# Dense products in pieces of 32 columns, and another order of all work, in a hybrid transformer kernel

## The reference

```python
x = x + s4_block(ln(x))      # gates i, f, o, s = products 256x256; h = f*h + i*s over all tokens; y = o*h; ln
x = x + ffn(ln(x))           # r = sigmoid(xr @ Wr.T); k = relu(xk @ Wk.T)**2; r * (k @ Wv.T); token shift
x = x + attention(ln(x))     # q, k, v, out: 256x256; 16 heads of 16; causal softmax over 4096 keys
x = x + ffn(ln(x))           # the same weights again
```

```python
scores = q @ k.T / 4; scores[key > query] = -inf
p = softmax(scores - scores.max(-1)); out = p @ v
```

## Time and profile before

| | before |
|---|---|
| median of 3 runs | 1784.84 us (1783.78 to 1785.69) |
| the profiled execution | 1785.71 us, span 1783.9 us |
| PE busy | 1742.3 us, 98% |
| DVE busy | 1533.4 us, 86% |
| ACT busy | 1312.9 us, 74% |
| POOL busy | 615.0 us, 34% |
| instructions | 34777, of them 12872 MATMUL |
| granted PE clock | full in nearly all slices |

### The profile page before, as it was taken

One profiled execution on the slowest core, in us unless ns is written; L12 is line 12 of the kernel. 1 busy time (PEld: TensorE's weight loads), 2 busy tenths in 40 slices (PEclk: granted clock), 3 DMA queues, 4 the chain that ended last, 5 costly groups with the idle time before them and its releaser, 6 DMA issues.

```text
span 1783.9 us, 34777 instructions
## 1 busy us (share of the span) xinstructions
PE 1742.3 (98%) x12872; PEld 761.8 (43%) x12872; DVE 1533.4 (86%) x3040; ACT 1312.9 (74%) x2660; POOL 615.0 (34%) x927
## 2 busy tenths in 40 slices
PE   8999999999999999999999999999999999999998
PEld 8766655533445433443433443433232333323214
DVE  6685994799999999999999998999999999999802
ACT  3345465588685678778688777688979788887894
POOL 4257868714337432333501524402010222120001
PEclk9999999999999999999999999999999999999999
DMA  4232121200002000020000002100002000000000
GB/s 110 59 65 53 34 49 39 53 11 18 24 12 53 29 12 6 19 47 6 23 6 13 7 24 29 29 6 1 1 25 28 17 12 7 13 2 8 1 1 12
DMA packets 56956, 43.01 MB, mean 24 GB/s; under 512 B 8788, under 2 KB 56788, under 8 KB 56788
## 3 DMA queue, kind: packets, MB, share of 16 engines
q1 hardware_dynamic: 54548, 39.75, 9.4%
q10 hardware_dynamic: 2240, 1.05, 0.4%
HBM read 24.00 MB, written 16.25 MB: 23 GB/s over the span
## 4 chain that ended last, share of the span: by engine, by line
PE 69%; DVE 19%; ACT 6%; issue 3%; POOL 2%; DMA 0%; ACTq 0%; SPq 0%; DVEq 0%; POOLq 0%
PE psum L1690 20%; DVE span_max L1433 14%; PE psum L1637 12%; PE psum L1669 12%; PE psum L1490 11%; PE psum L1496 10%; ACT probs L1188 3%; PE psum L1484 2%; ACT probs L1199 2%; PE psum L1699 1%; PE psum L1644 1%; DVE rows L1372 1%; DVE small L1290 1%; PE psum L1652 0%; POOL small L924 0%
## 5 line engine op out<-in xcount | busy, mean ns | idle before, releaser
L1433 DVE TENSOR_REDUCE span_max<-psum 128x1 f32<-128x512 f32 (+3 forms) x2304 | 1317.5, 639 | 84.0 <-PE psum L1637 57.7
L1188 ACT ACTIVATE probs<-psum 128x512 f32<-128x512 f32 (+3 forms) x2054 | 994.4, 572 | 144.2 <-PE psum L1669 138.2
L1690 PE MATMUL psum<-probs,v_aug 128*17 128x512 f32 (+3 forms) x4608 | 566.0, 563 | 1.9 <-POOL probs L1068 1.0
L1637 PE MATMUL psum<-k_stack,q_stack 48*128 48x512 f16 (+3 forms) x2304 | 515.7, 363 | 6.9 <-DVE span_max L1433 4.2
L1669 PE MATMUL psum<-q_stack,k_stack 50*128 50x512 f16 (+3 forms) x2304 | 516.9, 365 | 5.5 <-ACT probs L1199 1.2
L1669 PEld LDWEIGHTS psum<-q_stack,k_stack 50*128 50x128 f16 x2304 | 141.4, 93 | 436.5 <-ACT probs L1188 278.9
L1637 PEld LDWEIGHTS psum<-k_stack,q_stack 48*128 48x128 f16 x2304 | 160.1, 94 | 249.3 <-DVE span_max L1433 169.6
L1068 POOL TENSOR_SCALAR_AFFINE_SELECT probs<-probs 128x512 f32<-128x512 f32 x128 | 81.5, 642 | 429.8 <-ACT probs L1188 287.9
L1690 PEld LDWEIGHTS psum<-probs,v_aug 128*17 128x17 f32 x4608 | 76.6, 95 | 140.0 <-issue 119.1
L1199 ACT ACTIVATE probs<-psum 128x1024 f32<-128x1024 f32 (+3 forms) x125 | 116.4, 969 | 19.5 <-PE psum L1669 19.1
L1107 ACT ACTIVATE rows<-psum,cols 128x256 f32<-128x256 f32 x128 | 53.6, 470 | 91.3 <-PE psum L1490 90.9
(11 more groups left out here) (134 smaller groups left out, 1575.3 us busy)
## 6 DMA issues: line engine op xcount, KB each, us to landing
q_stack<-q_parts SPq DMA_DIRECT2D x192, 32.0 KB, 2.0
k_stack<-k_parts SPq DMA_DIRECT2D x42, 128.0 KB, 4.8
rows<-in_x SPq DMA_DIRECT2D x16, 256.0 KB, 2.8
q_parts<-rows SPq DMA_DIRECT2D x32, 128.0 KB, 1.9
k_parts<-rows SPq DMA_DIRECT2D x32, 128.0 KB, 2.0
out<-rows SPq DMA_DIRECT2D x16, 256.0 KB, 2.1
x_rows<-rows SPq DMA_DIRECT2D x14, 256.0 KB, 2.2
rows<-x_rows SPq DMA_DIRECT2D x14, 256.0 KB, 2.7
```

Source lines behind the costliest of these rows:

```text
L1188: act.activation(probs[:, tile % PROBS, i, q0:], bank(b)[:, q0:], ACT.Exp, scale=SCALE / QK_SCALE).then_inc(exp_done, 1)
L1433: nc.vector.tensor_reduce(span_max[:, s % SPAN_RING, row:row + 1, k0 // SPAN:k0 // SPAN + 1], bank(b)[:, 0:k1 - k0], AX.X, ALU.max).then_i ...
L1637: ins = nc.tensor.matmul(bank(b)[:, 0:k1 - k0], q_stack[row:row + SCORE_ROWS, s % Q_RING, u, qt * P:(qt + 1) * P], k_stack[row:row + SCORE ...
L1690: ins = nc.tensor.matmul(pv_bank[32 * h:32 * h + VW, q0:], v_aug[:, j, g * HG + h, :], probs[:, tile % PROBS, h, q0:], start=(j == 0), sto ...
```

## The change

1. In `channels_out` and `tokens_out` each product with 128 weight columns becomes four products with 32, each into its own 32 partitions of the same bank. The moving operand, the result and the number of bytes read for each product stay; it is read by four instructions in place of one. 896 products become 3584 (in MATMUL records 1792 become 7168).
2. `DIVISION` tells the planner that the products now have P V's shape.
3. The numbers of the planner change, and with them the order on every engine. `AHEAD` and `LEAD` become so large that they no longer hold anything back; `MAX_AHEAD` stays 2. `TOGETHER` is 0: two banks are taken at once only if both are ready.

```diff
+COLUMNS = 32
-MOST = {"max": 4, "scores": 5, "job": 5}
-KEPT = 1
+MOST = {"max": 4, "scores": 6, "job": 4}
+KEPT = 2
-AHEAD = 36199
-LEAD = 18.25
-NEAR = 0
-SOON, TWO = 0, -3100
+AHEAD = 1273693
+LEAD = 129438.363
+NEAR = -4100
+SOON, TWO = 0, -3700
-WORTH = {"max": 3000, "dve": 1.6, "scores": 2950, "act": 1.953, "half": -2700, "pv": 1200, "stay": -11650,
+WORTH = {"max": 2957.1, "dve": 1.615, "scores": 2300.4, "act": 1.51376, "half": -12007.3, "pv": -8025.2,
...
-TOGETHER = 100
+TOGETHER = 0
-DIVISION = {"shift": "pv"}
+DIVISION = dict.fromkeys(("shift", "f", "i", "s", "o", "r", "k", "kv", "q", "kk", "v", "proj"), "pv")
             def channels_out(b, w, src, e):
                 for k in range(CT):
-                    ins = nc.tensor.matmul(bank_chan(b)[:, e], w[:, k, e * P:(e + 1) * P], src[:, k],
-                                           start=(k == 0), stop=(k == CT - 1))
+                    for c in range(0, P, COLUMNS):
+                        ins = nc.tensor.matmul(bank_chan(b)[c:c + COLUMNS, e],
+                                               w[:, k, e * P + c:e * P + c + COLUMNS], src[:, k],
+                                               start=(k == 0), stop=(k == CT - 1))
                 return ins
 
             def tokens_out(b, w, src, j):
                 for k in range(CT):
-                    ins = nc.tensor.matmul(bank_tok(b)[:, j], src[:, k, j * P:(j + 1) * P], w[:, k],
-                                           start=(k == 0), stop=(k == CT - 1))
+                    for c in range(0, P, COLUMNS):
+                        ins = nc.tensor.matmul(bank_tok(b)[c:c + COLUMNS, j],
+                                               src[:, k, j * P + c:j * P + c + COLUMNS], w[:, k],
+                                               start=(k == 0), stop=(k == CT - 1))
                 return ins
```

More of the change, by code:

```diff
@@ L91 @@
 MAX_AHEAD = 2
-AHEAD = 36199
-LEAD = 18.25
-NEAR = 0
-SOON, TWO = 0, -3100
+AHEAD = 1273693
+LEAD = 129438.363
+NEAR = -4100
+SOON, TWO = 0, -3700
 REDUCE, EXP = 600, 480
-WORTH = {"max": 3000, "dve": 1.6, "scores": 2950, "act": 1.953, "half": -2700, "pv": 1200, "stay": -11650,
-         "two": -5450, "ring": -8700, "last": -10200, "job": -900, "age": 0.001, "same": 2700, "after": -4350,
-         "rest": 1050}
+WORTH = {"max": 2957.1, "dve": 1.615, "scores": 2300.4, "act": 1.51376, "half": -12007.3, "pv": -8025.2,
+         "stay": -4435.6, "two": -14292.2, "ring": -23714.7, "last": -26096.1, "job": 1809.8, "age": 0.0001,
+         "same": 8710.7, "after": 92.2, "rest": 1738.6}
 PE_SEEN, ACT_SEEN, DVE_SEEN, POOL_SEEN = 210, 180, 150, 150
```

## The result

| | before | after |
|---|---|---|
| median | 1784.84 us | 1769.72 us (1766.57 to 1770.74, 5 runs) |
| ratio | | 0.991, 95% interval 0.9896 to 0.9924 |
| profiled execution | 1785.71 us, span 1783.9 | 1769.91 us, span 1768.2 |
| last reduction ends | 1686.5 us | 1670.3 us |
| from there to the end | 97.4 us | 97.9 us |

What follows compares the result with a forecast made beforehand. PE (98% busy), with DVE at 95% in the middle, was taken as near its limit; -10.4 - 4.7 - 0.8 - 3 + 2.5 = -16.4 us on 1785.7 gave 1769.3, forecast as 1768 us, range 1747 to 1790.

Steps and rivals of the forecast that it cites:

- The bound: Whole program: PE busy 98% of the span, DVE 95% from 400 to 1600 us, both close to their limits.
- The pace of a piece: Layers' products on PE: a lone job takes 0.98 us in place of 1.06, a chained one stays at 0.86.
- Starts, changes of shape, halves: PE's list: fixed costs of starting and leaving runs -10.4 us, fewer lopsided halves -4.7, seven transposes gone -0.8.
- DVE fed earlier, -3 us: Reductions: 32 us of DVE's work lies earlier; DVE's late excess falls from 9 to 3 us, half counted.
- The last step, +2.5 us: ACT's final step: 9 more exps behind the last maximum, 42 full double exps in place of 57, +2.5 us.
- Issue time: PE's 5376 more MATMULs and as many loads cost issue time from 31 ns each; up to +363 us, 2131 us; chance 0.04.
- Slower by balance: From 400 to 1300 us maxima take DVE from the layers' small instructions, PE waits; 1798 us at 30 more; chance 0.12.

Runs made afterwards that it cites:

- dve_light: The changed kernel with each reduction reading only half of its columns: 1745.56 us, ratio 0.9779 to the kernel before.
- together100: The changed kernel with TOGETHER at 100 as before in place of 0: 1772.41 us, ratio 0.9921 to the kernel before.
- told_old_worths: The kernel before with products in four pieces and the planner told they have P V's shape, its worths as before: 1871.18 us, ratio 1.0483.
- shape_unknown: The changed kernel with the planner not told that jobs have P V's shape, so in another order: 1876.26 us, ratio 1.0504 to the kernel before.
- moving64: The changed kernel with each product also cut along the moving operand, 64 columns in place of 256: 1971.95 us, ratio 1.1045 to the kernel before.
- moving128: The changed kernel with each product also cut along the moving operand, 128 columns in place of 256: 1780.33 us, ratio 0.9974 to the kernel before.

## Why the prediction was right, step by step

- **The bound.** PE's list, with DVE close behind. Right, and dve_light shows how close: a DVE with a third less work gives 24 us, up to 7 of them by the clock.
- **The pace of a piece.** P V's price was taken: 0.98 us for a lone job, 0.865 for a chained one. Measured 1.00 and 0.865. The lone job is 0.135 and not 0.115 us above the chained one; 14 ns of that is the load, since 32 columns load in 109 ns and 17 in 95.
- **Starts, changes of shape, halves.** -10.4 - 4.7 - 0.8 = -15.9 us. The finer list says -16.9, and in the trace it came.
- **DVE fed earlier, -3 us.** Right in kind and too small: the last reduction ends 16 us earlier, and the waits after 1600 us fell by about 9 us. But the step stopped there. In the middle the waits rose by 10.5 us, which the sum had not, and only 3 of them are DVE's. The forecast had -0.5 us for all waits together (-3 and +2.5), and they came to +1.2, up to 1.9 of it by the clock. That the number was met so closely is luck: a rise and a fall of some 10 us, neither foreseen at that size, cancel.
- **The last step, +2.5 us.** 97.9 us in place of 97.4 from the last reduction to the end. The step was priced 2 us too high; together100, which takes more pairs together, gained nothing.
- **Rivals.** Issue time had 0.04 and was priced at up to 363 us. Its condition, 31 ns an instruction, fails by a factor of two at least: 15 ns in the worst row. The page "TensorE: Matmul & The Clock Gate" of the Trainium skill (Part 2) gives 62 ns for a MATMUL without hardware decoding. PE does not run at that pace here: by it a job of 64 MATMULs would need 4 us (an estimate from the page's figure), and moving64 does a lone one in 1.03. Issue does come at a price, but at twice to four times the changed kernel's instructions: moving128 and moving64 stop for it. Slower by balance had 0.12. Here I was lucky rather than right: told_old_worths and shape_unknown show that a new order can cost 5% where this one gives 0.5%, and nothing in my argument (runs counted, reductions by position) would have told them from the changed kernel. Nor did it price the clock, which takes up to 38 and 55 us of these two. For told_old_worths the same method said 1788 us and the chip 1871.

## What to carry to other kernels

An fp32 product can be issued in columns of 32 for nothing where its neighbours have that shape, and it saves the part of the first weight load that nothing covers, 0.06 us for each start here; count the starts before expecting more. Leave room for the instructions: at 27 ns each there was no stop, below 15 ns PE ran dry. A list of one engine's work, priced from starts in the trace, predicts well what an edit of the instructions does in a given order, and badly what a new order does: look there for a stretch in which the second engine runs dry, and for the clock that PE is granted after its own gaps. When two kernels differ by a few us, compare their granted clocks before naming an engine. Worths of a planner may belong to the costs that they were found with; one change of the costs alone lost 2.5% here.

## What the runs showed of the hardware that I had not expected

- PE keeps 64 MATMULs and 64 loads of a lone job within 1.03 us, but a long row of them runs at 15 ns an instruction on average: PE stops every 127 pairs, 3.9 us apart, in step with the 16.4 KB packets of the instruction queue, with 64 moving columns (stops of 1.6 to 2.0 us) and with 128 (0.2 to 0.3 us) alike.
- A load of fp32 weights lasts 95, 109, 136 and 189 ns on average for 17, 32, 64 and 128 columns.
- With DVE busy 95% of a stage that lasts 1200 us, a third less work for it took only 17 to 24 us off the whole program, clock included.
- The same kernel, dve_light, took 1745.3 to 1745.6 us with a mean granted clock of 1.000 and 1751.3 us with 0.998.
